# Layer 1 of a two-layer kernel: a pair's gate logits in the turn in which its rows are turned, its gates in the next turn, and the norms of the seventh and eighth pair one turn later

## The reference

```python
xn = _layernorm(x)                       # layer 1; x comes out of layer 0
q, k, v = xn @ wq.T + bq, xn @ wk.T + bk, xn @ wv.T + bv
s = softmax(q @ k.T * scale) @ v         # inside each sequence
logits = xn @ w_gate.T                   # 8 per row
topk_vals, topk_idx = top_k(logits, 2)
gates[row, topk_idx] = softmax(topk_vals)
hmid = gelu(einsum('th,eih->tei', xn, w_fc))
out = einsum('teh,te->th', einsum('tei,ehi->teh', hmid, w_proj), gates)
x = x + s * silu(out)
```

## Time and profile before

| | us |
|---|---|
| median of 3 runs (lowest, highest) | 444.33 (443.17, 444.63) |
| the profiled execution | 446.48 |
| its span | 444.7 |

### The profile page before, as it was taken

How to read it: one execution, slowest core, us unless ns; L and a number is a source line. 1 busy time by engine, 2 the same in 40 slices (tenths; PEclk the granted TensorE clock), 3 DMA queues, 4 the chain that set the end, 5 groups by cost and what they waited for, 6 DMA issues and landing times. The chain is left out here.

```text
span 444.7 us, 8741 instructions
## 1 busy us (share of the span) xinstructions
PE 384.2 (86%) x2604; PEld 347.4 (78%) x2604; DVE 311.8 (70%) x1113; ACT 256.5 (58%) x504; POOL 304.1 (68%) x364
## 2 busy tenths in 40 slices
PE   2928976995699999997999999897997999779994
PEld 1716965894299999996999998785986988679884
DVE  7987678779147666763746684964589989898453
ACT  2403214421047676762676666457987987789884
POOL 7967777777777777771777777837777777407820
PEclk9975989797789999995999999998999999999999
DMA  8989994111356667536567665331211111101301
GB/s 262 385 214 304 300 405 178 54 49 52 112 176 217 216 217 220 197 123 221 155 209 224 200 197 169 105 115 47 55 49 51 47 53 49 37 1 49 95 13 36
DMA packets 45902, 65.17 MB, mean 147 GB/s; under 512 B 8585, under 2 KB 23330, under 8 KB 45858
## 3 DMA queue, kind: packets, MB, share of 16 engines
q1 hardware_dynamic: 30322, 35.24, 25.4%
q0 software_dynamic: 8192, 16.79, 13.2%
q10 hardware_dynamic: 7344, 12.59, 7.8%
HBM read 28.93 MB, written 35.65 MB: 145 GB/s over the span
## 5 line engine op out<-in xcount | busy, mean ns | idle before, releaser
L556 POOL DMA_INDIRECT slot_rows<-xn_tok,slot_of x128 | 128.0, 1000 | 42.3 <-issue 38.6
L570 POOL DMA_INDIRECT onehot<-expert_rows,slot_of x64 | 64.9, 1014 | 34.5 <-issue 18.9
L570 POOL DMA_INDIRECT route_tmp<-expert_rows,slot_of x64 | 65.6, 1024 | 19.5 <-issue 19.5
L1466 DVE TENSOR_TENSOR act<-sg,ps 128x384 f32<-128x384 f32 x48 | 26.5, 553 | 54.6 <-ACT sg L1052 54.3
L763 PE MATMUL ps<-w_dn,actT 96*128 x384 | 51.2, 277 | 1.3 <-ACT zeros L1061 1.3
L763 PEld LDWEIGHTS ps<-w_dn,actT 96*128 96x128 f32 x384 | 46.8, 192 | 1.7 <-issue 1.7
L1052 ACT ACTIVATE sg<-ps 128x384 f32<-128x384 f32 x48 | 23.5, 490 | 39.8 <-PE ps L772 39.8
L772 PE MATMUL ps<-w_gu,raw_pr 128*128 x192 | 39.0, 350 | 0.2
L772 PE MATMUL ps<-w_gu,raw_fc 128*128 x192 | 37.8, 342 | 0.7 <-ACT raw_fc L1046 0.3
L1061 ACT COPY zeros<-ps 128x512 f32<-128x512 f32 x48 | 28.1, 586 | 14.9 <-PE ps L763 14.6
L772 PEld LDWEIGHTS ps<-w_gu,raw_pr 128*128 128x128 f32 x192 | 34.1, 206 | 0.8 <-issue 0.7
(11 more groups left out here) (244 smaller groups left out, 924.5 us busy)
## 6 DMA issues: line engine op xcount, KB each, us to landing
slot_rows<-zeros SPq DMA_DIRECT2D x12, 1024.0 KB, 12.4
rows<-slot_rows SPq DMA_DIRECT2D x48, 256.0 KB, 2.9
expert_rows<-zeros ACTq DMA_DIRECT2D x48, 256.0 KB, 2.3
x_tok<-in_L_attn_x_dram SPq DMA_DIRECT2D x8, 256.0 KB, 5.9
slot_rows<-xn_tok,slot_of POOLq DMA_INDIRECT x128
out_dram<-w_gu SPq DMA_DIRECT2D x16, 128.0 KB, 1.8
w_dn<-in_L_ffn_w_down_dram SPq DMA_DIRECT2D x1, 1536.0 KB, 16.6
onehot<-expert_rows,slot_of POOLq DMA_INDIRECT x64
```

Of the source, the lines that this page charges most:

```text
L556: g.indirect_dma_start(out=slot_rows[r], out_offset=bass.IndirectOffsetOnAxis(ap=slot_of[:, n:n + 1], axis=0), in_=xn_tok[:, r * HT + t, : ...
L570: g.indirect_dma_start(out=gath[b % 4][:, j, :], out_offset=None, in_=expert_rows[r], in_offset=bass.IndirectOffsetOnAxis(ap=slot_of[:, n: ...
L1466: v.tensor_tensor(act[u][:].rearrange("p (a b) i -> p a b i", a=2), sg[u][:].rearrange("p (a b) i -> p a b i", a=2), ps[:, 1 + 2 * u:3 + 2 ...
```

## The change

It has three parts.

1. **Logits.** `gate_logits(p)` on PE moves from the middle of turn b+2 (between `project` and `expert_sum`) to the end of turn b+1 (behind `output`). Its copy on ScalarE moves from before `keep_values` in turn b+2 to behind `weigh_output` in turn b+1, and waits for PE's logits. `values` now waits for that copy.
2. **Gates.** `top_gates` stays in turn b+2 but stands before `finish` in place of behind it. `tanh_gates` and `make_gates` move from turn b+3 to turn b+2.
3. **Norms.** The seventh pair is normed in turn 9 in place of 8, the eighth in turn 11 in place of 10. The sums, the mix and all that hangs on the norm move with them.

```diff
-NORM_AT = {0: 3, 4: 4, 6: 5, 8: 6, 10: 7}
+NORM_AT = {0: 3, 4: 4, 6: 5, 9: 6, 11: 7}
...
                 if b + 1 < NSEQ:
                     project(b + 1)
-                if turned(b - 2) is not None:
-                    gate_logits(turned(b - 2))
                 if b:
                     expert_sum(b - 1, 1 - u, b == 1)
                 if place == 0 and b:
                     turn_gates(batch)
+                if turned(b - 2) is not None:
+                    pe.wait_ge(c_lgs, turned(b - 2) + 1)
                 if b + 1 < NSEQ:
                     values(b + 1)
...
                 output(b, u)
+                if turned(b - 1) is not None:
+                    gate_logits(turned(b - 1)).then_inc(c_lg, 1)
...
-                if turned(b - 2) is not None:
-
-                    sc.wait_ge(d_v, b + 2)
-                    copy_gate_logits(turned(b - 2))
                 if b + 1 < NSEQ:
                     keep_values(b + 1, 1 - u)
                 if b:
                     tanh_moe(b - 1, b == 1)
-                if b and gated(b - 1) is not None:
-                    tanh_gates(gated(b - 1))
+                if gated(b) is not None:
+                    tanh_gates(gated(b))
                 if turned(b + 1) is not None:
                     tanh_f(turned(b + 1))
                 if turned(b - 1) is not None:
                     copy_xn(turned(b - 1))
                 weigh_output(b, u)
+                if turned(b - 1) is not None:
+                    logits_between(turned(b - 1), turned(b - 1) + 1)
...
+                if gated(b) is not None:
+                    top_gates(gated(b))
                 if b:
                     finish(b - 1)
-                if b and gated(b - 1) is not None:
-                    make_gates(gated(b - 1))
                 if gated(b) is not None:
-                    top_gates(gated(b))
+                    make_gates(gated(b))
                 if turned(b) is not None:
                     norm1(turned(b))
```

## The result

| | us |
|---|---|
| changed kernel, median of 4 runs (lowest, highest) | 450.38 (448.83, 452.66) |
| kernel before, median of 4 runs | 444.48 |
| ratio, 95% interval | 1.0145 (1.0103 to 1.0187) |
| profiled execution, its span | 448.83, 447.1 |
| the same kernel again, on another occasion, median of 6 runs | 452.97, against 444.98 of before |

What follows compares the result with a forecast made beforehand. DVE was taken to bound the middle turns, a PE-ACT loop the end. Stretches of +1.99, −0.92, +1.19, −0.54 and +3.85 gave +5.6 us on 444.33: 449.9; own forecast +3.7 to +7.0 (448.0 to 451.3), range 446.8 to 451.9.

Steps and rivals of the forecast that it cites:

- The new wait: ACT's tanh_gates waits for same-turn gd in turns 2, 6, 8, 11, 13: scaling 1.55 us late, 0.8 more in turn 2.
- given as a sign: ACT's wait before L1157 in turns 2, 6, 8, 11 and 13: 1.2 to 2.5 us each, ended by gd.
- The logits: ACT waits for logits in turns 1, 5, 7, 10, 12: 0.35 us each, given back where PE bounds the next turn.
- The norms: Later norms relieve DVE in turns 8 to 10, nearly all taken by the gd wait: −0.54 us there.
- Turns 10 and 12, the term that was too small: Turns turning rows and gates together: 9.15 us plus 0.35 for the logits, 9.5 each.
- The rival with GpSimd: GpSimd's finishing stretches the last pair's make_gates beyond turn 14's 2.4 us slack: +7.5 us, 451.8; chance 0.1.
- The faster rival: gd ready by the output's end, so DVE's relief wins: −1.5 us, 442.8; chance 0.07.
- second rival: Waits partly hidden, 1.1 us per wait and 0.1 per logits copy: +2.3 us, 446.6; chance 0.16.

Runs made afterwards that it cites:

- e9: Changed kernel plus two unread TensorE products each in turns 10 and 12, and GpSimd waiting before its tenth sequence until the last gates are made: 450.59 us, 1.0144.
- e1: Changed kernel with top_gates moved to the head of its turn: 444.5 us, 1.0012 of the kernel before.
- e11: e6 run again, on one chip with e12: 442.4 us, 0.9976 of the kernel before.
- e3: Kernel before with only the logits moved; top, tanh, gates and norms as before: 445.86 us, 1.0036.
- e2: Changed kernel with the old norms (turns 8 and 10), so only logits and gates moved: 451.77 us, 1.0162 of the kernel before.
- e10: e6 with the old norms (turns 8 and 10): 445.88 us, 1.0054 of the kernel before.
- e4: Changed kernel plus two unread TensorE products before project in turn 10 and two before spread_gates in turn 12: 453.63 us, 1.0201 of the kernel before.
- e6: e1 with GpSimd made to wait before its tenth finished sequence until the last batch of gates is made: 441.5 us, 0.9932 of the kernel before.
- e7: e6 with the seventh pair normed in turn 8 as in the kernel before: 443.94 us, 0.9985 of the kernel before.
- e8: e6 plus two unread TensorE products in turn 10 directly behind hidden_of: 442.98 us, 0.9967 of the kernel before.
- e12: e8 run again, on one chip with e11: 441.24 us, 0.9925 of the kernel before.

## Why the prediction was right

The time was forecast at 449.9 and measured at 450.38 and, again, at 452.97. The direction and its cause were right; the sum was 2.4 us short over the turns (129.4, which e9's expectation has as 129.3, against 131.79), which the first measurement hid in the stage ahead of them. So the agreement within 0.5 us was luck: the second measurement, 8.0 us above the kernel before, is beyond the +7.0 of the forecast.

- *The new wait.* Forecast: five waits, the scaling at 2.69 behind the output's start, eight tiles 0.8 more. Measured 2.67 in turn 11. Turns 6, 11 and 13 took 9.35, 9.35 and 9.58 (forecast 9.3, 9.3, 9.5), turn 8 10.75 (10.8), turn 2 10.17 (10.06). e1 takes the wait away and these five turns lose 9.2 us. The waits seen in ACT's rows (2.48 to 3.31) were longer than the 1.2 to 2.5 given as a sign, though the start of the scaling was right. And their worth in the whole sum, 7.1 by the forecast (8.55 by its own terms, 5 × 1.55 + 0.8), was too small: e9 and e11, both at full clock through turn 13, differ by 120.24 − 111.80 = 8.4 us there.
- *The logits.* Forecast 0.35 in the turns that turn rows, given back behind them where PE bounds the next turn. Turn 1 took 9.45 in place of 9.10; turns 5 and 7 were at 8.53 and 8.52, for which I had 8.68. e3 puts the whole part at 0.3 us of the turns, and 1.4 in turn 15, which I had as before.
- *The norms.* Forecast: the relief of DVE is real, and nearly all of it is taken by the waits. Turn 4 was at 9.14 as laid out, without the 2.72 us for `rden`. e2 and e9, and e10 and e11, show both halves at turns 8 to 10: the later norms bring 30.35 − 29.38 = 1.0 us with the waits, and 30.53 − 27.84 = 2.7 without, of which a part is e10's clock in turn 9. That DVE was busy for only half the time in turns 11 to 13 was misread: it was 16.9 of 24.5 us, and half in turn 13 alone. It had room for the norms even so.
- *Turns 10 and 12, the term that was too small.* "I take 9.15 ... and 0.35 for the logits: 9.5" in turn 10 and "9.5 (as turn 10)" in turn 12. At full clock both lengths are exact: 9.50 and 9.51 in e9. But the sum took over the granted clock of 1.00 that the kernel before had in all these turns, its 2.58 us of idle PE between turns 8 and 9 included. In the changed one the clock fell after 2.0 and 2.4 us, and the lower level over some 5 us each time cost 1.03 and 1.60 us. These 2.63 us account for the 131.79 − 129.4 = 2.4 that were missing.
- *The rival with GpSimd.* It was priced as something on top of the waits. In the changed kernel `make_gates` was indeed stretched, by 1.3 us, but turn 14 has more slack than that and took 8.71. The collision counted where GpSimd had more left: with the wait gone (e1, +1.17), and in e4, where PE waited 2.07 us for it. In e1's order it went when GpSimd waited (e6).
- *The faster rival* had 442.8 for the case that `gd` is there in time. With top first, e1 measured 444.5, with turn 10's clock (+1.0) and GpSimd's collision (+1.2) on top of it; without the latter, e6 and e11 measured 441.5 and 442.4. Its condition was stated rightly, and the change didn't meet it. The rival's sum was too careful: it had −1.5 us over the turns, and e11 has −3.3.
- *A slip in the second rival.* A copy at 0.1 in place of 0.35 saves 0.25, not 0.2, so its sum is +2.1. No chance hangs on that.

What stays open is what decides whether PE's clock falls. The length of the idle stretch alone doesn't. Falls followed 1.60 us (turn 15 of e2, e3 and e10), 1.76 (e3, turn 9; e7, turn 7), 2.0 to 2.4 (the changed kernel, e4, e9), 2.5 and 2.6 (where turn 10 begins in e1 and e6) and 3.2 us (where turn 9 begins in e10). None followed 1.60 in turn 15 of the other kernels, 2.25 in turn 14 of e1, 2.53 where turn 10 begins in e11, or 2.58 in the kernel before. Filling the gap went with a full clock at that place in each kernel that tried it (e4, e8, e9, e12), but e11 shows that turn 10 can do without. So in turn 10 the filled kernels prove little by themselves; turn 12, which fell in both profiles of the changed kernel and in neither e4 nor e9, is the better evidence. That the lost 2.63 us are the clock's is shown by the durations; that the idle stretch is what lets it fall is likely, but not shown.

## What to carry to other kernels

A chain over several engines can be moved one turn nearer only if each link's result is there when the next engine comes to it. The engine that waits (here ScalarE, for a tanh of 0.2 us) has a queue behind it, and the wait's price is that of what stands there. Before such a move, read off when the producer is through in its own turn, counted from an event that both engines share. If it comes late, move the producer to the head of its turn together with the consumer; here that turned +8.0 us over the turns into −1.1 (123.79 to 122.73, e1), and with GpSimd's adds held back as well into −2.4 to −3.3 (e6, e11). And a sum of durations that were read at full clock can be 1.0 to 1.6 us short for a single idle stretch of TensorE; that 2.58 us of it cost the kernel before nothing is no proof for 2.0 us elsewhere. Last, count the turn behind the last one that was laid out, too: 1.4 us of three kernels were there.

## What the runs showed of the hardware

- The granted clock of TensorE went to its lower level for some 5 us after idle stretches of 1.6 to 3.2 us inside otherwise busy work, and a product that took 1.03 us took 1.91. After other stretches of 1.6 to 2.58 us it stayed at 1.00. With a pair of unread products (1.9 us) in the gap it stayed at 1.00 each time, but the fall came in a later gap of the same kernel in e4 and e9 (turn 14).
- Beside GpSimd's adds of 0.73 us, VectorE's steps of `make_gates` (0.16 to 0.19 us alone, on 128x32 and 128x4 elements) took up to 0.76 and ended with the add, also those with one input. The picking steps (L1542, L1545) on 128x8 elements weren't stretched, while `gd` right behind them took 0.36 to 0.49 in place of 0.17.
